# Five sampled units of each of three images by products under the next image's LSTM, in place of three by gathers

## The reference, cut to what matters

```python
x = x + _L0_conv_ref(_gn(x), ...)   # attention in 8 x 8 blocks with a halo of 3, 4 heads
x = x + _L1_conv_ref(_gn(x), ...)   # LSTM of 96 steps, hidden size 128, then a linear layer
x = x + _L2_conv_ref(_gn(x), ...)   # deformable convolution
x = x + _L3_conv_ref(_gn(x), M)     # 8 x 8 block transform
```

```python
offset = conv2d(x, p_w, p_b, 1, 1)
m = sigmoid(conv2d(x, m_w, m_b, 1, 1))
p = offset + p_n + base
...
x_off = g_lt * gather(qx_lt, qy_lt) + g_rb * gather(qx_rb, qy_rb) + g_lb * gather(qx_lt, qy_rb) + g_rt * gather(qx_rb, qy_lt)
x_off = x_off * m
...
return conv2d(x_off, conv_w, None, stride=KS, padding=0)
```

## Time and profile before

| what | value |
|---|---|
| time, median of 3 runs | 3617.43 us (3611.35 to 3619.76) |
| time of the profiled execution | 3624.01 us |
| its span in the profile | 3622.2 us |
| busy: PE, PEld, DVE | 2785.3 us, 2027.9 us, 2479.2 us |
| busy: POOL, ACT | 2380.0 us, 1263.4 us |
| POOL's gathers | 2403 instructions of nine for a unit, 267 units |

### The profile page before, as it was taken

The page is one execution under the profiler, slowest core; times in us unless marked ns, Lnnn a source line. Parts: engine busy times, 40 slices in busy tenths (PEclk is TensorE's granted clock), DMA queues, the critical chain, the costliest instruction groups (busy, mean ns, idle before and its releaser), DMA issues. The chain is left out here.

```text
span 3622.2 us, 59607 instructions
## 1 busy us (share of the span) xinstructions
PE 2785.3 (77%) x21833; PEld 2027.9 (56%) x21833; DVE 2479.2 (68%) x5480; ACT 1263.4 (35%) x3105; POOL 2380.0 (66%) x2445
## 2 busy tenths in 40 slices
PE   6979984885899748867998568668987376889882
PEld 4667763664676526646666346546665254555542
DVE  4754447985777669965777679756777675677763
ACT  4644433542433315523333145324333121222210
POOL 3200026777777777777777777777777777777774
PEclk9999996886899868876999779768999688999995
DMA  6622025764321346636212376543213432222211
GB/s 214 194 60 73 1 71 166 208 174 93 88 60 53 106 145 192 193 82 123 59 53 68 96 216 193 145 94 87 59 54 104 87 94 73 65 63 70 59 53 48
DMA packets 270803, 374.53 MB, mean 103 GB/s; under 512 B 109508, under 2 KB 181336, under 8 KB 269992
## 3 DMA queue, kind: packets, MB, share of 16 engines
q1 hardware_dynamic: 166688, 200.21, 19.2%
q0 software_dynamic: 76896, 157.64, 16.0%
q10 hardware_dynamic: 26928, 12.87, 1.6%
HBM read 270.08 MB, written 99.55 MB: 102 GB/s over the span
## 5 line engine op out<-in xcount | busy, mean ns | idle before, releaser
L769 POOL DMA_INDIRECT got<-sample_table,index x2403 | 2325.2, 968 | 1092.3 <-issue 726.6
L1618 PE MATMUL gates<-cells,row_hat 128*128 128x400 f32 x1782 | 653.3, 513 | 67.8 <-DVE spanned L1153 53.2
L1618 PEld LDWEIGHTS gates<-cells,row_hat 128*128 128x128 f32 x1782 | 332.7, 194 | 309.6 <-issue 84.2
L1175 DVE TENSOR_TENSOR got<-got,bank 128x864 f32<-128x864 f32 x267 | 279.6, 1047 | 242.5 <-DMA got<-sample_table,index 234.3
L852 ACT ACTIVATE pt<-gates 98x512 f32<-98x512 f32 x528 | 288.6, 594 | 325.8 <-PE gates L1726 304.7
L1826 PEld LDWEIGHTS gates<-hist,whh 128*128 128x128 f32 x2280 | 313.5, 205 | 138.7 <-DVE hist L1469 100.8
L1826 PE MATMUL gates<-hist,whh 128*128 128x96 f32 x2280 | 325.9, 290 | 53.8 <-DVE hist L1469 53.1
L1286 DVE TENSOR_REDUCE mx<-gates 128x2 f32<-128x392 f32 x576 | 295.5, 553 | 82.3 <-PE gates L1712 80.9
L1606 PE MATMUL bank<-turned,wout 128*128 128x96 f32 x1728 | 244.9, 304 | 131.5 <-DVE turned L1203 66.1
L1606 PEld LDWEIGHTS bank<-turned,wout 128*128 128x128 f32 x1728 | 239.0, 219 | 156.4 <-DVE turned L1203 110.5
L1712 PE MATMUL gates<-kst,qst 96*128 96x196 bf16 x1152 | 185.2, 278 | 119.7 <-DVE mx L1286 103.1
(11 more groups left out here) (188 smaller groups left out, 4791.6 us busy)
## 6 DMA issues: line engine op xcount, KB each, us to landing
kst<-k_parts SPq DMA_DIRECT2D x96, 441.0 KB
got<-sample_table,index POOLq DMA_INDIRECT x2403
qst<-q_parts SPq DMA_DIRECT2D x96, 288.0 KB
k_parts<-kp SPq DMA_DIRECT2D x24, 882.0 KB
k_parts<-kp SPq DMA_DIRECT2D x24, 588.0 KB
q_parts<-qp SPq DMA_DIRECT2D x24, 576.0 KB
spread<-locations ACTq DMA_DIRECT2D x84, 144.0 KB, 3.9
sample_table<-tab SPq DMA_DIRECT2D x12, 784.0 KB
```

Of the source, the lines that this page charges most:

```text
L769: pool.indirect_dma_start(out=got[:, g % RING, n, :], out_offset=None, in_=tables[p], in_offset=bass.IndirectOffsetOnAxis(ap=at, axis=0)). ...
L1175: dve.tensor_tensor(corners, corners, w[:, :, 0:3].unsqueeze(3).to_broadcast([P, NTAP, 3, C]), ALU.mult).then_inc(weighted, 1)
L1618: mm = pe.matmul(sums_of(s, h), row_hat[:, 3 * v % HATS + n // TAPS3, t, n % TAPS3, :], cells[:, t, C // 2 * h:C // 2 * (h + 1), :].rearra ...
```

## The change

Five units of each of the images 0 to 2 are done by products (units 62 to 66 of the image) in place of three (60 to 62), so that 261 units are gathered in place of 267. The dense steps under each LSTM rise from 27 to 45, still in steps 14 to 95. In a step of the LSTM the dense sums stand behind the point's parts in DVE's program, where they stood ahead of them, and a half's sum stands in the step in which PE fills it, where it stood in the next. The numbers behind `DUE` are new, with `BEGUN` for the six points ahead of attention's loop. The row positions of a unit are turned on PE unit by unit and stored by one transfer for an image. `dsamp` and `located` share memory, so that ACT waits in `prepare(p)` until the products' units of the image before are turned.

```diff
-        stages += [(6 + 3 * NU, ATTENDED[p]), (W, STEPPED[p]), (prep_points(p), PREPARED[p])]
+        stages += [(6, BEGUN[p]), (3 * NU, ATTENDED[p]), (W, STEPPED[p]), (prep_points(p), PREPARED[p])]
...
-ATTENDED = (0, 28, 96, 167)
-STEPPED = (0, 59, 127, 199)
-PREPARED = (0, 68, 138, 210)
-SHARED = (213, 216, 230)
+BEGUN = (0, 7, 77, 148)
+ATTENDED = (0, 26, 97, 168)
+STEPPED = (0, 61, 133, 204)
+PREPARED = (0, 72, 143, 214)
+SHARED = (215, 216, 230)
...
-DENSE_GROUPS = tuple((p, 20) for p in range(LAST)) + ((LAST, 6), (LAST, 11), (LAST, 16), (LAST, 21))
-DENSE = {UNITS * p + GUNITS * k + i: GUNITS * d + i for d, (p, k) in enumerate(DENSE_GROUPS) for i in range(GUNITS)}
-DENSE_UNIT = {v: uu for uu, v in DENSE.items()}
+LUNITS = 5
+BATCHES = tuple((p, 62, LUNITS) for p in range(LAST)) + tuple((LAST, first, GUNITS) for first in (18, 33, 48, 63))
...
-    n = t - FIRST_PIECE + 1
-    return min(max(4 * (n // 2) + 3 * (n % 2), 0), PIECES * GSTEPS)
+    n, whole = max(t - FIRST_PIECE + 1, 0), W - 1 - FIRST_PIECE
+    return min(PIECES * USTEPS * (8 * (n // 2) + 5 * (n % 2)) // (4 * whole + 1), PIECES * USTEPS)
...
-        sums += [half[0] + 1, half[1] + 1, half[1] + 2]
-    hats = [FIRST_HAT + NTAP * n + i for n in range(3 * GUNITS) for i in range(2 * KTILES)]
+        sums += [half[0], half[1], half[1]]
+    hats = [FIRST_HAT + (W - 1 - FIRST_PIECE) * n // (3 * LUNITS) + i for n in range(3 * LUNITS) for i in range(2 * KTILES)]
...
-                for i, d in enumerate(groups_of(p)):
-                    act.wait_ge(rows_turned, d + 1)
-                    wait(act, dense_summed, GSTEPS * p)
-                    act.activation(located[:, i, :], located_ps[i], ACT.Copy).then_inc(rows_copied, 1)
+                if p > 0:
+                    act.wait_ge(samp_turned, DENSE_UNIT[LUNITS * p - 1] + 1)
+                for i, (first, last) in enumerate(banks_of(p)):
+                    act.wait_ge(rows_turned, banks_upto(p) + i + 1)
+                    act.activation(located[:, P * first:P * last], located_ps[i][:, 0:P * (last - first)], ACT.Copy).then_inc(rows_copied, 1)
...
-                    while p > 0 and dense_done < 3 * GSTEPS * p and SUM_AT[dense_done - 3 * GSTEPS * (p - 1)] <= t:
+                    point()
+                    while p > 0 and dense_done < 3 * USTEPS * p and SUM_AT[dense_done - 3 * USTEPS * (p - 1)] <= t:
                         dense_sum(dense_done // 3, dense_done % 3)
                         dense_done += 1
-                    point()
...
-                for i, d in enumerate(groups_of(p)):
-                    pe.wait_ge(dense_ready, d + 1)
-                    pe.transpose(located_ps[i], cell_rows[:, i].rearrange("p u n a -> p (u n a)"),
-                                 ident[:, :]).then_inc(rows_turned, 1)
+                pe.wait_ge(dense_ready, groups_of(p)[-1] + 1)
+                for i, (first, last) in enumerate(banks_of(p)):
+                    for u in range(first, last):
+                        mm = pe.transpose(located_ps[i][:, P * (u - first):P * (u - first + 1)], cell_rows[:, u].rearrange("p n a -> p (n a)"),
+                                          ident[:, :])
+                    mm.then_inc(rows_turned, 1)
```

More of the change, by code:

```diff
@@ L178 @@
 LAST = B - 1
-DENSE_GROUPS = tuple((p, 20) for p in range(LAST)) + ((LAST, 6), (LAST, 11), (LAST, 16), (LAST, 21))
-DENSE = {UNITS * p + GUNITS * k + i: GUNITS * d + i for d, (p, k) in enumerate(DENSE_GROUPS) for i in range(GUNITS)}
-DENSE_UNIT = {v: uu for uu, v in DENSE.items()}
+LUNITS = 5
+BATCHES = tuple((p, 62, LUNITS) for p in range(LAST)) + tuple((LAST, first, GUNITS) for first in (18, 33, 48, 63))
+BATCH_OF = [(d, u) for d, (_, _, n) in enumerate(BATCHES) for u in range(n)]
+DENSE_UNIT = [UNITS * BATCHES[d][0] + BATCHES[d][1] + u for d, u in BATCH_OF]
+DENSE = {uu: v for v, uu in enumerate(DENSE_UNIT)}
 GATHERED = [uu for uu in range(B * UNITS) if uu not in DENSE]
 ORDINAL = {uu: g for g, uu in enumerate(GATHERED)}
+GROUPS_PLACED = sorted({uu // GUNITS for uu in GATHERED})
+PLACING = {next(uu for uu in GATHERED if uu // GUNITS == k): n for n, k in enumerate(GROUPS_PLACED)}
+PLACED_FOR = {uu: GROUPS_PLACED.index(uu // GUNITS) + 1 for uu in GATHERED}
 DUNITS = len(DENSE)
 GSTEPS = GUNITS * NTAP
-LSTEPS = GSTEPS * LAST
+USTEPS = LUNITS * NTAP
+LSTEPS = USTEPS * LAST
+LATEST = sum(p == LAST for p, _, _ in BATCHES) - 1
+IMAGE_UNITS = [sum(n for of, _, n in BATCHES if of == p) for p in range(B)]
 DSTEPS = DUNITS * NTAP
@@ L196 @@
 SPREADS = 2
-SAMPLES = 2 * GUNITS - 1
-LATER_HATS = sum(p == LAST for p, _ in DENSE_GROUPS) - 1
-LOCATIONS = GUNITS * NTAP * CELLS
+SAMPLES = 5
+LOCATIONS = NTAP * CELLS
 FAR = 1000.0
@@ L228, in dense_points @@
     steps, done, last = [LSTEPS] * len(due), LSTEPS, -1
-    for k in (k for p, k in DENSE_GROUPS if p == LAST):
-        usable = [i for i in points if i > last and due[i - 1] < PARTS * (UNITS * LAST + GUNITS * k + 1)]
+    for first in (first for p, first, _ in BATCHES if p == LAST):
+        usable = [i for i in points if i > last and due[i - 1] < PARTS * (UNITS * LAST + first + 1)]
         for m, i in enumerate(usable):
@@ L253, in network @@
     planes = [nc.dram_tensor(f"planes{p}", [C, H, PADW + 1], F32, kind="Internal").ap() for p in range(B)]
-    locations = [nc.dram_tensor(f"locations{d}", [LOCATIONS, P], F32, kind="Internal").ap() for d in range(len(DENSE_GROUPS))]
+    locations = [nc.dram_tensor(f"locations{p}", [IMAGE_UNITS[p], LOCATIONS, P], F32, kind="Internal").ap() for p in range(B)]
     k_parts = nc.dram_tensor("k_parts", [2, P, NTERM, NB * KEYS], BF16, kind="Internal").ap()
@@ L355, in network @@
             mx1 = sb("mx1", [P, CH, NTAP], where=a2)
[L356 to L359, removed]
+            cell_of = sb("cell", [P, LUNITS, NTAP], where=a2)
+            other_of = sb("other", [P, LUNITS, NTAP], where=a2)
+            inner_of = sb("inner", [P, LUNITS, NTAP], where=a2)
+            cell_rows = sb("cell_rows", [P, max(IMAGE_UNITS), NTAP, CELLS], where=a2)
         with ExitStack() as a3:
@@ L546, in hats_of @@
         def hats_of(d):
-            late = d - LAST
-            return first_hat if late <= 0 else later_hat[:, late - 1]
+            n = BATCHES[d][2]
+            return first_hat[:, 0:n] if d <= LAST else later_hat[:, d - LAST - 1]
         def sums_of(s, h):
@@ L555, in groups_of, with banks_of, banks_upto @@
         def groups_of(p):
-            return [d for d, (of, _) in enumerate(DENSE_GROUPS) if of == p]
+            return [d for d, (of, _, _) in enumerate(BATCHES) if of == p]
+        def banks_of(p):
+            return [(first, min(first + 4, IMAGE_UNITS[p])) for first in range(0, IMAGE_UNITS[p], 4)]
+        def banks_upto(p):
+            return sum(len(banks_of(of)) for of in range(p))
         block = ctx.enter_context(nc.Block())
@@ L921, in lstm @@
                 if p > 0:
-                    for v in range(GUNITS * (p - 1), GUNITS * (p - 1) + SPREADS):
+                    for v in range(LUNITS * (p - 1), LUNITS * (p - 1) + SPREADS):
                         load_spread(v)
@@ L1547, in pixel_math @@
                 for d in groups_of(p):
-                    if first <= GUNITS * DENSE_GROUPS[d][1] < first + N:
+                    if first <= BATCHES[d][1] < first + N:
                         dense_positions(d)
@@ L1612, in dense_piece @@
                 if (h, t) == (0, 0):
[L1613 to L1614 removed]
+                    if s % USTEPS == 0 and s <= LSTEPS:
+                        pe.wait_ge(cells_in, 16 * KTILES * CELLS * (s // USTEPS + 1))
                     pe.wait_ge(hat_ready, KTILES * (3 * v + n // TAPS3 + 1))
@@ L1938, in prepare @@
                 combine()
-                wait(pe, dense_read, 2 * GSTEPS * p)
+                wait(pe, dense_read, 2 * USTEPS * p)
                 for i in range(EARLY):
```

65 lines of the change are left out of this document (33 added, 32 removed).

## The result

The kernel after takes 3674.45 us (median of 4 runs, 3667.25 to 3679.73), the one before 3614.64 us beside it: a ratio of 1.0163 [1.0140, 1.0186], some 60 us slower. The forecast was slower by 25 us. The profiled execution takes 3679.73 us, 55.7 more than the one of before, over a span of 3677.9.

A forecast was written before the change was run, and what follows sets the result against it. POOL bounds the kernel before; after, the late stages hold it: transform 1 ends at 3003 us, plus 5, 607 for the remaining gathers and 32 gives 3647, or 3642 us against the median; range 3595 to 3675.

The forecast's parts named there:

- end of transform 1: End of the stages before POOL's last stretch: moves by +57 us, from 2946.4 to 3003 us.
- the stages' slack: DVE's waits for gathered data in attention 1 to 3 and prepare 2 and 3 all come back: -89 us.
- attention, fewer units: Fewer units in attention's loop, 3.35 us of DVE each: -35 us over three images; bounds nothing and -45.
- prepare: Fewer gathered units in prepare 2 and 3, -14 us; larger hats for images 0 to 2, +7 us.
- LSTM: 18 more dense steps of PE work under each LSTM: +66 us each, three times; bounds +50 and +82.
- transforms 0 and 1: One unit each instead of three, -13 us; image 3's turns ahead of the first transform, +3: -10 us.
- the third rival: DVE becomes the bound in the LSTM: 25 us more an LSTM, 3716 us against the median; chance 0.08.
- signs named: LSTM 1 about 418 us, PE busy 96% or more from step 14, attention's data waits gone; wrong under 405 us.
- Balance: LSTMs longer by 50 to 58 us, or shorter attention; equal time at +56 to +60; chances 0.13 faster, 0.14 same.
- Behind transform 1: POOL's last stretch: 54 units, 486 gathers at 1.25 us, 607 us, after some 5 us for the first slot.
- The first rival: POOL stays the bound, products fit between the LSTM's recurrences by the weight loads' share: 3548 us against the median; chance 0.10.
- The order of the sums: DVE's sums behind the point's parts in LSTM steps delay no `hist` that PE could use earlier: nothing.

The follow-up runs named there:

- eight-tap run: Kernel before with eight gathers a unit instead of nine from the seventh unit on: 3475.69 us, ratio 0.9610.
- two thirds: Kernel after without the middle one of the three products of each half step under the LSTMs: 3598.79 us, ratio 0.9959 to the kernel before.
- light sums: Kernel after with DVE's sums of products under the LSTMs cut to one column of 25: 3668.41 us, ratio 1.0143 to the kernel before.
- sums ahead: Kernel after with the sums of products put back ahead of the point's parts in an LSTM step: 3691.05 us, ratio 1.0221 to the kernel before.
- late hats: Kernel after with ACT's image 3 loads moved behind transform 0 and first row hats behind transform 1: 3653.36 us, ratio 1.0103 to the kernel before.
- units ahead: Kernel after, last two image 2 units weighed in prepare 3, two image 3 units in each transform, image 3 batches three units later: 3635.26 us, ratio 1.0071.
- the control with late hats: Kernel before with ACT's loads and row hats for image 3 moved behind transforms 0 and 1: 3615.00 us, ratio 1.0005.

## Why the prediction was right in direction and short by more than half

The mechanism was the one forecast: POOL's saving is there, POOL stands at its ring, and the end of transform 1 plus 55 units of gathers plus 31.5 us is the span. The time lay inside the range, at its very end. The sum to the end of transform 1 was off by 25 us, and its terms are set apart by the eight-tap run, in which no stage waits for POOL (sums over the three images, us):

| term of the sum | forecast | measured | from |
|---|---|---|---|
| the stages' slack | -89 | -66 | transform 0 at 2814.9 in the eight-tap run, 2881.1 before |
| attention, fewer units | -35 | -10 | 887.5 after, 897.0 in the eight-tap run |
| prepare | -7 | -15 | 274.3 after, 289.3 in the eight-tap run |
| LSTM | +198 | +179 | 1248.3 after, 1069.4 in the eight-tap run |
| transforms 0 and 1 | -10 | -5 | 60.3 after, 65.3 before |
| end of transform 1 | +57 | +82 | 3028.5 after, 2946.4 before |

The rows measured add up to 83; attention 1 began 1.3 us sooner in the kernel after than in the eight-tap run.

**Attention is the step that failed**, in two terms at once. The prediction took DVE for its limit ("the engine that others wait for") and priced a unit less at 3.35 us and a wait less at its full length; it named the other bound, nothing, "if PE is the bound there", and chose the wrong end. Once the data are there in time, PE is as late as DVE: with six units fewer attention gets 1.0 us a unit, and in attention 1 about half of DVE's waits stayed in the eight-tap run, as waits for PE. In the kernel after DVE's waits for gathered data are gone from attention, as forecast; what it waits for there, in attention 1, is PE, and PE waits for DVE in turn:

```profile
DVE mx L1306 <- PE gates L1732: 19.2, 16, 3.2
DVE osb L1327 <- PE bank L1691: 6.7, 5, 1.9
```

```profile
PE gates L1732 <- DVE mx L1306: 25.4, 10, 12.3
```

So DVE alone is not the limit there. That PE's work is, is not shown: no run took work off PE alone in attention.

The two terms together made the sum 48 us too low: 25 by the units, 23 by the waits, 17 of these in attention and 6 in prepare. The 25 is the less sure of them. In the profile of the kernel after attention 1 took 299.0 us; in the five others with its due numbers there (two thirds, light sums, sums ahead, late hats, units ahead) 292.2 to 292.7. The three attentions together take 877 to 888 us in these six, 882 on average: 9 to 20 us less than the 897.0, 15 on average.

**The LSTM** was over-sized, by 19 us in three. Measured were +56, +59 and +64 us, against +66. Steps 14 to 95, where the sum put all of it, are 61.5, 65.1 and 58.1 us longer, from `hist` to `hist`: 13 of the 19 us. In LSTM 1 PE's busy time rises by 70 us there (forecast 73.7), and its idle time falls from 23.8 to 15.0. Most of the other 6 us lie ahead of step 14, where no pieces stand and the granted clock differs: 60.6 us for 65.4 in LSTM 1, at 0.75 for 0.60, but 71.6 for 65.5 in LSTM 3, at 0.55 for 0.58. That PE bounds the steps, and not DVE, is shown by the light sums; the third rival, DVE, is out at five units, though not far off, as the run with two thirds of the pieces shows. Of the signs named, PE is busy 96% from step 14 on, DVE's waits for data are gone from attention, and LSTM 1 takes 408.6 us where about 418 was said and under 405 would have been wrong.

**Balance** was worked out to come at +56 to +60 us for an LSTM; the LSTMs came out there, at +59.5 on average, and the time was 60 us longer, not equal. What was wrong was the other side of the balance, above all attention.

**Transforms 0 and 1.** The prediction took two units each off DVE; but DVE stood idle there for ACT's standard deviation, 19.9 us in one wait, and 16.0 us before. Taking work off an engine that waits brings little: 5 us. **Prepare** gave 8 us more than forecast. That the sum to the end of transform 1 was off by 25 us and not by twice as much is luck: the LSTMs and prepare erred the other way, by 19 and 8 us.

**Behind transform 1** POOL had 55 units left, not 54, and needed 617.9 us instead of 5 + 607: some 6 us. With the 25 us that is the 31 us between the forecast span of 3647 and the measured one. POOL waits 165 us after its first gather instead of 95: its stretch from the first gather to the last is 33 us longer than forecast, and the gathers take 37 us less, 1.262 each without the waits. The forecast's 1.278 held before's own 20 us of waits, which is about half of these 37. The profiled execution lies 5 us above its runs' median, as that of before lay 6.6 above its own.

**The first rival**, POOL stays the bound, fails with the rule that spoke for it. PE's weight loads are 239 of 345 us in steps 14 to 95, 69%, as before (194 of 282), and PE is busy 96%. Taking pieces away shortened the steps by 28 us, and taking DVE's work away by 3: the room was what PE's busy share left. The Trainium skill, Perfetto Trace Analysis, "Identifying the Most-Contended Engine", judges PE's headroom by the former share, together with the share of the peak arithmetic (not worked out here), and calls the latter no good measure of how close PE is to its peak; in these steps the latter was the better guide. The same section names the engine of the highest occupancy as the most contended: between its first and last gather before, POOL is busy 2325 of 3072 us, 76%, DVE 72%, and PE's weight loads take 54%. That POOL bounds the kernel before, the control with late hats bears out.

**The order of the sums** was costed at nothing and is worth some 17 us in the run that puts the sums back.

## What to carry to other kernels

A wait that goes away is worth its length only if no other engine is nearly as late; before counting it, make the data early in a run of its own and see what the engine waits for next. When the bound is about to pass from one engine to another, every term of the stages that were off the path starts to count, and each must be read anew: units that cost 3.35 us of DVE cost 1 us of time in attention. And a gain too big to be hidden may pay in part: four units instead of five, with one queue put in order, gave 0.9% where five cost 1.6%.

## What the runs showed that was not expected

Attention 1 has the same instructions in six of these kernels, and takes 299.0 us at a mean granted clock of 0.76 in the kernel after and 292.2 at 0.81 with the hats late (a mean over stretches at 1.2 and at 2.4 GHz), with PE busy 231.6 and 217.2 us: one profile against another carries 7 us there. And a convolution queued on PE can hold a table: in prepare 3 it waits for DVE's addition of rows, and the last turns of `sample_table` stand behind it (PE's timeline of the kernel after):

```profile
2900.88 4.13 PE L1626 MATMUL bank<-turned,wout 128*128 128x96 f32 x18 [15.84 <-DVE x L1229]
2904.80 1.16 PE L1941 MATMUL gates<-ident,near 128*98 128x128 f32 x6
```
